# Moving the first 17 events of the second attention's maxima into the projection stage

## What is computed

```python
xn = _layernorm(x, axis=-1)
qkv = jnp.einsum('bnh,hm->bnm', x, w_qkv)
q, k, v = jnp.split(qkv, 3, axis=-1)
q = rmsnorm(q, q_gamma)
k = rmsnorm(k, k_gamma)
q = q * cos + rotate_half(q) * sin
k = k * cos + rotate_half(k) * sin
mask = (q_idx >= k_idx) & (q_idx - k_idx <= WINDOW)
scores = jnp.einsum('bhqd,bhkd->bhqk', q, k) / np.sqrt(HD)
scores = jnp.where(mask[None, None, :, :], scores, NEG)
attn = jax.nn.softmax(scores, axis=-1)
out = jnp.einsum('bhqk,bhkd->bhqd', attn, v)
```

## Time and profile before

| | us |
|---|---|
| median of three runs | 1545.77 (1545.43 to 1546.54) |
| the profiled execution | 1546.45 |
| its span, first to last instruction | 1544.7 |
| outside the span | 1.7 |
| projection stage, about | 637 to 780 |
| attention stage, about | 780 to 1287 |
| TensorE busy over the span | 1469.8 (95%) |

### The profile page before, as it was taken

How to read it: one execution, slowest core, us unless ns; L and a number is a source line. 1 busy time by engine, 2 the same in 40 slices (tenths; PEclk the granted TensorE clock), 3 DMA queues, 4 the chain that set the end, 5 groups by cost and what they waited for, 6 DMA issues and landing times. The chain is left out here.

```text
span 1544.7 us, 23513 instructions
## 1 busy us (share of the span) xinstructions
PE 1469.8 (95%) x6981; PEld 1061.2 (69%) x6981; DVE 1040.6 (67%) x2926; ACT 744.4 (48%) x1268; POOL 481.6 (31%) x705
## 2 busy tenths in 40 slices
PE   5999999999999999899989999999999998898998
PEld 4778788888776787788855555555555545687776
DVE  6553666666657757887767986666668974568592
ACT  5623566566563433433324555555555562235561
POOL 0000677777610334323221221211212213054062
PEclk9999999999999999999968999999999999999999
DMA  5002222222110424367797415225135027744021
GB/s 185 1 1 77 88 75 78 109 75 78 52 48 7 138 100 120 118 193 199 197 234 286 90 39 120 63 66 120 35 92 120 13 63 212 240 170 157 20 90 14
DMA packets 107125, 161.53 MB, mean 105 GB/s; under 512 B 12353, under 2 KB 63697, under 8 KB 100625
## 3 DMA queue, kind: packets, MB, share of 16 engines
q1 hardware_dynamic: 101868, 153.64, 33.0%
q10 hardware_dynamic: 4516, 5.38, 1.0%
q0 software_dynamic: 640, 1.31, 0.5%
HBM read 117.44 MB, written 42.87 MB: 104 GB/s over the span
## 5 line engine op out<-in xcount | busy, mean ns | idle before, releaser
L2123 ACT ACTIVATE l_pt<-banks 128x1024 f32<-128x1024 f32 (+3 forms) x288 | 218.5, 811 | 139.7 <-PE banks L1998 137.8
L2195 DVE CUSTOM_DVE_ANT_0 stage<-banks,l_edges 128x384 f32<-128x384 f32 (+3 forms) x384 | 201.6, 542 | 71.2 <-issue 69.8
L2035 PE MATMUL banks<-l_pt,l_v 128*64 128x512 f32 (+3 forms) x1152 | 221.8, 506 | 1.9 <-POOL l_pt L2093 1.9
L724 POOL TENSOR_TENSOR ex_hl<-ex_h,ex_hh 128x512 fp32r<-128x512 f32 x128 | 165.7, 1301 | 81.1 <-ACT ex_hh L692 80.9
L2092 POOL TENSOR_TENSOR l_turn<-l_before 128x2 f32<-128x2 f32 x192 | 38.6, 201 | 384.4 <-ACT l_pt L2123 373.5
L757 DVE SCALAR_TENSOR_TENSOR ex_rw<-banks,ex_wb 128x512 f32<-128x512 f32 x128 | 88.3, 691 | 79.1 <-PE banks L75 79.0
L2198 DVE TENSOR_REDUCE l_mx<-banks 128x1 f32<-128x384 f32 (+1 forms) x208 | 113.0, 544 | 41.2 <-PE banks L1976 40.5
L2035 PEld LDWEIGHTS banks<-l_pt,l_v 128*64 128x64 f32 x1152 | 69.3, 138 | 91.3 <-issue 68.0
L692 ACT ACTIVATE ex_hh<-ex_h 128x512 fp32r<-128x512 f32 x128 | 80.9, 632 | 103.7 <-DVE ex_h L765 102.5
L73 PE MATMUL banks<-ex_xlh,ex_wh 128*128 128x512 f32 x256 | 101.6, 397 | 2.1 <-DVE ex_rw L757 2.1
L74 PE MATMUL banks<-ex_xll,ex_wh 128*128 128x512 f32 x256 | 99.8, 390 | 0.0
(11 more groups left out here) (454 smaller groups left out, 3467.3 us busy)
## 6 DMA issues: line engine op xcount, KB each, us to landing
ex_wb<-gates_by_expert SPq DMA_DIRECT2D x16, 1024.0 KB, 4.8
l_v<-layer_v SPq DMA_DIRECT2D x8, 1024.0 KB, 17.4
layer_qk<-qkv_yh SPq DMA_DIRECT2D x30, 256.0 KB, 3.2
layer_qk<-qkv_yl SPq DMA_DIRECT2D x30, 256.0 KB, 3.6
layer_v<-qkv_vs SPq DMA_DIRECT2D x15, 512.0 KB, 4.8
ex_ws<-ew_in SPq DMA_DIRECT2D x16, 384.0 KB, 5.1
l_q<-layer_qk SPq DMA_DIRECT2D x12, 512.0 KB, 7.7
l_k<-layer_qk SPq DMA_DIRECT2D x12, 512.0 KB, 13.6
```

The lines of the kernel that those rows point to most:

```text
L724: pool.tensor_tensor(hl[:, k % RING, :], h[:, k % RING, :], raw(hh[:, k % RING, :]), ALU.subtract).then_inc(hl_done, 1)
L2035: last = pe.matmul(bank[h * 2 * HD:(h + 1) * 2 * HD, (qa - b * BT) * P:(qz + 1 - b * BT) * P], v[par][:, kt, h, :], pt[:, step_part(b, j), ...
L2123: act.activation(pt[:, step_part(b, j), :, 0:width], G.banks[:, 2 * slot:2 * slot + 2, 0:width], ACT.Exp, scale=scale).then_inc(p_done, 1)
L2195: dve.tensor_tensor_reduce(cutoff[:, n % 4, 0:width], G.ps[5 + n % MB][:, 0:width], masked, 1.0, NEG, ALU.add, ALU.max, mx[:, h, m, c:c + ...
```

## The change

1. The first 17 events move into the projection stage. In the passes of tiles 7 to 15, TensorE gets one event behind `queries(t)` and one behind `keys(t)`: two chunks a tile in tiles 7 to 14 and the rows event in tile 15. All use one bank, 5: each waits until VectorE has reduced the one before it (`a_red`). The first waits for `first_in` 96, that is all six transfers of `first_pair(0)`, and event 10, in tile 12, for 192.
2. VectorE reduces an event behind `turned(t, 0)` and one behind `inverses(t)`, and builds the mask and fills before tile 6. ScalarE copies the rows ahead of the last `value`.
3. The values lose their second bank: all but tile 1 use bank 4, and `values(t)` waits for the copy of tile t-1, not t-2.
4. The attention stage's prologue no longer holds events.
5. `headsel` and its three instructions go; the maxima's tiles move into room of the first layer's `kvb`.

SyncE's program is as it was, `first_pair` with it.

```diff
-    with nc.sbuf_tensor("headsel32", [P, NC, P], F32) as headsel, nc.Block() as block:
+    with nc.Block() as block:
...
-            pool.memset(headsel[:, :, :], 0.0)
...
-            dve.tensor_copy(G.headsel[:, :, :], headsel[:, :, :])
...
+    BEGIN = 7
+    G.MADE = 2 * (NT - 1 - BEGIN) + 1
+    made = [(t, n) for n in range(G.MADE) for t in [BEGIN + n // 2]]
+    MAXIMA = 5
...
+        def value_bank(t):
+            return 5 if t == 1 else 4
...
+            def maximum(n):
+                u, kind, h = sequence[n][:3]
+                bank = G.ps[MAXIMA]
+                if kind == "chunk":
+                    _, _, _, m, c, k0, k1 = sequence[n]
+                    if n == 0:
+                        pe.wait_ge(v_sb, 2)
+                    if h == 0 and m == 0 and c == 0:
+                        pe.wait_ge(first_in, 96 * (u + 1))
+                    wait(pe, a_red, n)
+                    qt = u * BT + m
+                    pe.matmul(bank[:, 0:(k1 - k0) * P], G.q0[0:3 * HD, h, qt * P:(qt + 1) * P], G.k0[0:3 * HD, h, k0 * P:k1 * P],
+                              start=True, stop=True).then_inc(a_mm, 1)
+                else:
+                    pe.wait_ge(a_red, n)
+                    pe.wait_ge(m_done, 1)
+                    for m in range(BT):
+                        last = pe.matmul(bank[0:HD + 2, m * P:(m + 1) * P], G.mrow[:, m, 0:HD + 2], G.identr[:, :],
+                                         start=True, stop=True)
+                    last.then_inc(mr_mm, 1)
...
-                wait(pe, v_sb, t - 1)
+                wait(pe, v_sb, t if t >= 3 else t - 1)
...
                 queries(t)
+                maxima(t, 0)
                 keys(t)
+                maxima(t, 1)
                 transposes(t - 1)
...
             high(NT - 1)
+            act.wait_ge(mr_mm, 1)
+            for h in range(2):
+                act.activation(G.q0[3 * HD:3 * HD + 2, h, 0:TB], G.ps[MAXIMA][h * HD:h * HD + 2, :], ACT.Copy).then_inc(mr_sb, 1)
             value(NT - 1)
...
             for t in range(1, NT):
+                if t == BEGIN - 1:
+                    masks()
                 turned(t, 0)
+                maxima(t, 0)
                 means(t)
                 turned(t, 1)
                 inverses(t)
+                maxima(t, 1)
                 low(t - 1)
...
-                    yield i, n
+                    if n >= G.MADE or not isinstance(i, int) or i > 0:
+                        yield i, n
```

More of the change, by code:

```diff
@@ L1434, in stage_qkv @@
     G.qk_out, G.v_out = qk_out, v_out
+    G.maxima_sems = [G.lasting_sem("l1_" + n) for n in ("a_mm", "a_red", "nm", "mh", "m", "mr_mm", "mr_sb")]
+    a_mm, a_red, nm_done, mh_done, m_done, mr_mm, mr_sb = G.maxima_sems
+    mask_done = G.sem("qkv_mask")
+    plans = [Plan(b) for b in range(NB)]
+    sequence = maxima_order(plans)
+    BEGIN = 7
+    G.MADE = 2 * (NT - 1 - BEGIN) + 1
+    assert sequence[G.MADE - 1] == (0, "rows", 0)
+    made = [(t, n) for n in range(G.MADE) for t in [BEGIN + n // 2]]
+    MAXIMA = 5
     with ExitStack() as stack:
@@ L1542, in values @@
                 else:
-                    product(t, "v", 4 + t % 2).then_inc(v_mm, 1)
+                    product(t, "v", value_bank(t)).then_inc(v_mm, 1)
             pe.transpose(G.ps[7][0:NT, 0:P], G.score[:, :], G.ident[:, :]).then_inc(score_mm, 1)
@@ L1688, in value_low, with reduce, negate, masks @@
                 dve.tensor_tensor(G.wqh[:, part], G.vraw[:, c, :], raw(G.wql[:, part]), ALU.subtract).then_inc(vwl_done, 1)
+            def reduce(n):
+                u, kind, h = sequence[n][:3]
+                if kind == "rows":
+                    return
+                _, _, _, m, c, k0, k1 = sequence[n]
+                width = (k1 - k0) * P
+                dve.wait_ge(a_mm, n + 1)
+                if k1 == u * BT + m + 1:
+                    dve.memset(G.carry[:, n % 4, :], 0.0)
+                    dve.tensor_tensor_reduce(G.stage[:, n % 4, 0:width], G.ps[MAXIMA][:, 0:width], mask[:, BANK - width:BANK],
+                                             1.0, NEG, ALU.add, ALU.max, G.mx[:, h, m, c:c + 1]).then_inc(a_red, 1)
+                else:
+                    dve.reduce_max(G.mx[:, h, m, c:c + 1], G.ps[MAXIMA][:, 0:width], axis=AX).then_inc(a_red, 1)
+                if n + 1 == plans[0].chunks:
+                    negate()
+            def negate():
+                dve.wait_ge(a_red, plans[0].chunks)
+                dve.tensor_reduce(G.nm[:, :, :], G.mx[:, :, :, 0:max(len(c) for _, c in plans[0].maxima)], AX, ALU.max,
+                                  negate=True).then_inc(nm_done, 1)
+                dve.wait_ge(nm_done, 1)
+                rows = G.mrow[:, :, :].rearrange("p m (h n) -> p h m n", h=2)
+                dve.tensor_copy(rows[:, :, :, 0:1], G.nm[:, :, :].unsqueeze(3)).then_inc(mh_done, 1)
+                dve.wait_ge(mh_done, 1)
+                dve.tensor_tensor(rows[:, :, :, 1:2], G.nm[:, :, :].unsqueeze(3), raw(rows[:, :, :, 0:1]),
+                                  ALU.subtract).then_inc(m_done, 1)
+            def masks():
+                dve.memset(mask[:, 0:BANK - P], 0.0)
+                dve.memset(G.mx[:, :, :, :], NEG)
+                dve.tensor_copy(mask[:, BANK - P:BANK], G.lower[:, :]).then_inc(mask_done, 1)
+                dve.wait_ge(mask_done, 1)
+                dve.tensor_copy(G.mrow[:, :, :].rearrange("p m n -> p (m n)"), mask[:, 0:BT * 2 * HD]).then_inc(mask_done, 1)
+                dve.wait_ge(mask_done, 2)
+            def maxima(t, k):
+                for n in [n for at, n in made if at == t][k:k + 1]:
+                    reduce(n)
             dve.wait_ge(G.tables, 4)
@@ L1729, in __init__, with maxima_order @@
         self.back = back
+def maxima_order(plans):
+    sequence, late = [], []
+    for u in range(2 * NB):
+        chunks = [(u, "chunk", h, m, c, k0, k1) for h in range(2)
+                  for m, (qt, cuts) in enumerate(plans[u % NB].maxima) for c, (k0, k1) in enumerate(cuts)]
+        sequence += chunks[:6] + late + chunks[6:]
+        late = [(u, "rows", 0)]
+    return sequence + late
 def sums_of(dram, b0, b1):
```

33 lines of the change are left out of this document (17 added, 16 removed).

## The result

The changed kernel takes 1563.89 us (median of four runs, 1561.54 to 1568.78) against 1546.1 for the kernel before in runs beside it: the ratio is 1.0118, with an interval from 1.0106 to 1.0130. It is 1.2% slower: against 1545.77 that is 18.2 us, with an interval from 16.4 to 20.1. Its profiled execution took 1562.35, with a span of 1560.7, and that is the one to set against the sum of the prediction (1562.95 before it was shifted to the median).

A forecast was written before the change was run, and what follows sets the result against it. TensorE, busy 132.78 of 133 us, bounds the projection stage. 1546.45 - 4.5 + 11.3 + 1.7 + 3.4 + 3.6 + 1.1 + 0.5 - 0.6 = 1562.95, 1562.3 against the median; range 1557.0 to 1567.5.

The forecast's parts named there:

- the hold in tile 7: Behind queries(7), ahead of keys(7), TensorE waits with the first moved event for first_pair(0)'s transfers: +11.3 us, bounds 11.1 and 11.4.
- The restart: After the idle time in tile 7 the matmuls run at half clock for a stretch: +1.7 us, bounds 0 and 3.5.
- The matmuls: The moved events' own matmuls, row matmuls included, lie on TensorE's full projection stage: +3.4 us.
- The wait for the one bank: In tiles 8 to 11, 13 and 14 the second event waits for VectorE's reduction: 6 x 0.6 = +3.6 us, bounds 1.5 and 5.
- The second load: In tile 12, event 10 behind queries(12) waits for keys landing at about 740.5: +1.1 us, bounds 0 and 2.
- Value bank, tail and barrier: At the projection stage's end values(14) waits 0.9 us, values(15) 0.15, and ScalarE ends 0.5 later than SyncE: +0.5 us.
- The selector: In the first stage, without the selector VectorE ends before SyncE: -0.6 us, bounds -0.8 and 0.
- The start of attention: Prologue of 9.5 us removed, but ScalarE's DMA issues hold the first exponential: -4.5 us, ends -3 and -5.3.
- the first: Rival: no hold in tile 7, reductions in time, attention starts the whole 9.5 us earlier: 1539.6 us, chance 0.03.
- The third: Rival: waits in each projection pass keep the clock low for longer: 1565.7 us for two more stretches, 1567.4 for three, chance 0.09.
- The fourth: Rival: the single value bank costs 0.9 us in each of 11 passes, tiles 5 to 15: +9.9, 1572.2 us, chance 0.03.
- The second rival: The change's loads are met: no hold, no restart, no second load, all else as forecast: 1548.2 us, chance 0.03.

The follow-up runs named there:

- the third experiment: Changed kernel with first pair's loads ahead of the stores of tiles 4, 8 and 12, and each tile's second event behind transposes(t-1): 1546.38 us, ratio 0.9986.
- its repetition: The third experiment unchanged, run once more on another chip, against the kernel before: 1546.15 us, ratio 0.9993.
- the first experiment: Changed kernel with the first pair's queries and keys loaded behind the stores of tiles 4, 8 and 12 instead of 5, 9 and 13: 1555.65 us, ratio 1.0048.

## Why the prediction was right

The forecast was that the hold in tile 7 outweighs the prologue; it did, and the terms can be read one by one. The shift of each matmul of the projection stage against its counterpart before gives them (start after minus start before): -0.5 on entry, +11.4 at `keys(7)`, +13.3 at full clock again, +21.2 at `keys(15)`, +21.65 at attention's first matmul. The -0.5 on entry is not the selector: the shift is -0.54 at TensorE's first matmul, +1.28 at 601 us, and then falls by 1.8, because the profiled execution of the kernel before ran at half clock from 604.97 to 608.44 and that of the changed kernel did not.

- **The hold in tile 7**: 11.3 expected. The idle time is 11.47, and with the exposed start of the event 11.7. It came from SyncE's row for the loads and their landing time of 5.0; after, they were issued 0.5 earlier and landed in 4.8 to 5.2. The estimate by the Trainium skill (DMA: Bandwidth & Descriptors, Anatomy of one DMA), 2.7 us less, does not agree with these rows.
- **The restart**: 1.7 expected from the earlier trace rows, 1.9 by the shift. That it came at all could not be read from those rows (see the last section).
- **The matmuls**: 3.4 expected, 3.2 by the shifts. A first event of a tile costs 0.14 to 0.23, the rows event 0.27.
- **The wait for the one bank**: 3.6 expected as six times 0.6. The six waits are 0.28 to 0.38 of idle time; with the weight load behind it each is some 0.55, and 3.3 in all. The reading of VectorE's rows was right: the reduction stands behind `turned` and TensorE meets it halfway.
- **The second load**: 1.1 expected, 1.6 by the shift (1.39 of idle time). It is the term with the largest relative error; it was a difference of four small numbers.
- **Value bank, tail and barrier**: 0.5 expected; 0.9 and 0.2 on TensorE, less the 0.67 by which it had been waiting for the barrier, 0.46.
- **The selector**: -0.6 expected, -0.5 at TensorE's first matmul in the changed kernel, -0.7 alone. No run's time can tell it.
- **The first layer**: no term was given to it; 1.1 us between 116 and 601 us, as above. Its cause is open.
- **The start of attention**: -4.5 expected, -5.0 at the first product with values. What is late next was named wrongly: not the values (landed at 815.7), but TensorE itself, which works through the thirteen events until 817.3. Another 0.7 is gained up to the rows event at 841.26, where the kernel is 16.0 us behind before: the clock is full again 32.3 us into the stage instead of 39.8. So the start of attention gives 5.7, more than the bound of 5.3. Over the whole stage, from its first matmul to the end of its last product, it is 5.0 (507.98 to 502.93), and the changed kernel's trace has a stretch of 3.4 us at half clock from 1069.7 in it that the other has not. The prediction named an attention stage shorter by more than 5.3 as a sign of being wrong: the start of the stage passes that, the whole of it does not.

The sum of the measured ones is 21.65 - 5.0 = 16.7 at the first product with values, against 16.5 forecast. That they are so near is in part luck: without the half clock at 605 us in the one trace and not in the other it would be some 18.5, about the 18.2 of the medians. The mechanism does not hang on it, since hold, restart, waits and second load were each read by themselves, and the experiments took them away. Of the rivals, the first is out by the hold of 11.47 us. The third did not come: in the projection stage the clock fell only with the hold. The fourth was shown to be nothing by the value bank alone. The median of 1563.89 is 1.5 above the profiled execution; the four runs differ by 7 us, and the two slowest have the lowest mean clock (0.975 and 0.976), but the fastest has 0.980 where the profiled one has 0.983.

The second rival, costed at 1548.2, is the experiment with the loads in time: its ratio on the median of 1545.77 gives 1548.6. What the prediction missed is at the start of attention: it looked for what is late next only up to the first product with values, while a load that is needed 24 us later bounds the gain. In the changed kernel that made little difference (VectorE waited 0.31 us for it).

## What to carry to other kernels

Before work is moved ahead on the engine that is always busy, look up in the trace when the engine that feeds it issues its loads; the loads have to move as well, and ahead of that engine's stores, or the wait costs many times the work. Where a wait for a shared bank is as short as 0.4 us, one block of other matmuls between producer and consumer removes it. And when a gain at a stage's start is gone some tens of microseconds later, look for the next thing there that is tied to the same event of the stage before, here a 1 MB load behind the last stores; taking away the nearer waits one by one then gives nothing, and can cost, as the longer wait further on can bring a half clock with it.

## What the runs showed of the hardware

- The clock after idle time: the granted clock is 1.0 or 0.5 of full speed in these traces. At 604.5 to 607.7 us TensorE comes out of an idle time of 2.44 to 2.48 us in all fourteen traces. In seven of them some 3.4 us at half clock follow, in the other seven none, whichever kernel it is (the third experiment has none, its repetition has it); it costs 1.8 us. Within the idle time of 11.47 us the clock fell 2.2 us after its start, and 4.2 us at half clock followed it; one of 2.70 us in the first experiment was followed by none. The length of the idle time alone did not decide it.
- Runs of one kernel differ by up to 9 us, and part of it goes with the mean granted clock: the third experiment took 1541.13 us at 0.986 and 1548.37 at 0.979, the kernel before 1550.66 and 1550.96 at 0.978. But the third experiment also took 1541.08 at 0.983, and its repetition 1546.74 at the same. Ten to twelve runs left intervals of 0.2 to 0.3%.
- In two traces a VectorE cast of 128x8 waited 1.2 and 2.0 us until GpSimd's fill of 2x4096 ended, while a reduction of 128x16 beside the same fill did not.
- A 1 MB load behind 4.9 MB of others on SyncE's queue landed 20.4 to 21.5 us after its issue in all fourteen traces, whether it was issued at 798 or 819 us.
